# A gated attention and expert block on one core: the pieces of SP's, GpSimd's, ScalarE's, TensorE's and VectorE's lists set in another order

## The chip, the cores and the metric

One core of one Trainium2 chip. The metric is the device time of one launch in microseconds (us). The clock of TensorE has two levels here, 1.2 and 2.4 GHz; the profile gives the granted share of the higher one. In the tables PE is TensorE, DVE VectorE, ACT ScalarE, POOL GpSimd and SP the engine that only issues DMAs.

## The reference, cut to what matters

```python
# x (4, 512, 512), ctx (4, 512, 128), all float32; T = 4 * 512 rows
def mixer(h, adj, Wq, Wk, gamma_raw):                 # h = ctx, adj = layernorm(x)
    Q, K = heads(h @ Wq.T), heads(h @ Wk.T)           # 4 heads of 32
    sim = einsum('bhnd,bhmd->bnm', Q, K) / (sqrt(32) * 4)
    thr = top_k(sim, 153)[0][:, :, -1:]               # 153 = 0.3 * 512
    A = sigmoid(sim) * (sim >= thr)
    A = (A + swapaxes(A, -1, -2)) * 0.5
    g = sigmoid(gamma_raw)
    return (1 - g) * adj + g * A
def ffn(h, ...):                                      # h = layernorm(x), 8 experts, 2 of them per row
    shared = silu(h @ sg) * (h @ su) @ sd
    top_val, top_idx = top_k(h @ router, 2)
    probs = zeros.at[rows, top_idx].set(sigmoid(top_val))
    gate, up = split(einsum('etd,edf->etf', probs.T[:, :, None] * h, gate_up_w))
    return shared + einsum('eti,eid->etd', silu(gate) * up, down_w).sum(0)
x = x + tanh(g_xattn) * mixer(ctx, layernorm(x), ...)
x = x + tanh(g_ffn) * ffn(layernorm(x), ...)
```

## The kernel before, in words

The four blocks b of 512 rows go through the same stages, each of four tiles i of 128 rows. Every stage is a small helper, and each engine has a list of helper calls, written out by hand, that it works off strictly in order. Helpers of different engines meet in semaphores alone. So the order of the work is the five lists (SP's, GpSimd's, ScalarE's, TensorE's and VectorE's), and a helper that waits holds everything behind it in its list.

**Scores.** turn_ctx/turned_ctx (L926, L578) and turn_q/turned_q (L934, L582) make the operands, sim_tile (PE, L940) a 128x512 tile of scores, sim_of (ACT, L586) copies it to SBUF.

**Threshold search.** sim_stats (DVE) and spread (POOL) give a first probe; then four rounds k of count (DVE, L1385) and sign (ACT, L591), which count the entries above the probe for different tiles (block 0: two each; other blocks: DVE one, ACT three), and move (DVE, L1392), which sets the next probe. last_count, best_below and threshold (DVE, L1404 to L1436) end it; check_search stands on PE and DVE, read_bad on ACT. best_below works in two tiles of tmp which the one-hots use too, so it waits for the table before.

**Mixing.** value (ACT, L598) makes tanh and identity of four tiles, mask_sim (DVE, L1457) multiplies by the mask, affine (ACT, L620) scales x (with row_stats, row_affine on DVE, root_of_rows on POOL), turn_a (PE, L949) transposes the masked scores, add_own and add_turned (DVE) add them. mixed_stats, mixed_spread, normal_in (DVE), root_of_mixed (POOL) and normal (ACT, L626) are the second layer norm. The PE's turn_x2 (L960) and ACT's turned_x2 (L634) turn its rows.

**Routing and plan.** route, turn_logits (PE), turned_logits (ACT, L644); pick_experts (DVE, L1502) takes the logits, probs (ACT) and weigh_experts (DVE) the weights, which store_payload (SP) writes. rank_pairs (PE), rank_tokens (DVE, L1547) and one_hots (DVE, L1562: eight operations at L1569 and eight at L1572) are the operands of table (PE, L989), add_table (DVE) adds it up. count_pairs, order_columns, name_rows (PE) and sum_pairs, choose_columns, place_columns, read_plan (DVE) turn it into lists of rows. This is done twice: a first plan after blocks 0 and 1 gives the first nine groups of 128 rows (EARLY = 9), the second, after block 3, the other thirty. gather(t) (POOL, L477) fetches group t by an indirect DMA when rows and payload of its blocks are in DRAM.

**Jobs.** There are 55 jobs j. S jobs (the shared expert, one per tile of 128 rows) are j = 0 to 7, 12 to 15 and 19 to 22; M jobs (one expert on one gathered group t) are j = 8 to 11 (t = 0 to 3), 16 to 18 (t = 4 to 6) and from 23 on. Each is up(j) (PE, L1029), silu_of(j) (ACT), gate(j) (DVE, L1633), for an M job turn_h(j) and turned_h(j), then down(j) (PE, L1061), y_of(j) (ACT), and shared(j) or scatter(t) (POOL), which adds to the output in DRAM. up(j) waits for gate(j - 2); an S job's gate(j) waits for down(j - 2). An M job needs turn_rows(t) (PE, L1020) and turned_rows(t) (ACT) before. warm(n, count) (PE, L909) is `count` matmuls on ones that compute nothing.

From job 27 on the lists are loops of one M job a turn, alike in both kernels.

```python
            def best_below(b):
                ...
                if tables[0]:
                    dve.wait_ge(table_ps, tables[0])
            def gate(j):
                dve.wait_ge(silu_ready, j + 1)
                ...
                else:
                    if j >= 2:
                        dve.wait_ge(y_ps, j - 1)
```

## Time and profile before

| what | value |
|---|---|
| median of 3 runs | 416.89 us (416.11 to 417.19) |
| the profiled execution, its own time | 417.2 us |
| its span, first to last instruction | 415.5 us |
| mean granted clock | 0.976 |
| DVE, ACT, POOL busy | 182.1, 188.1, 132.0 us |
| SP's queue, GpSimd's queue | 28.40 MB, 24.81 MB |
| one job's 32 small matmuls of an S up / 4 matmuls of a down | 3.6 to 3.8 / 1.72 us |
| count of one tile, move, DVE | 0.74, 0.35 us |
| row_stats, sim_stats, DVE | 3.0, 2.0 us |
| last_count, best_below, threshold, DVE | 3.1, 4.8, 0.7 us |
| mask_sim or add_own, DVE | 2.7 us |
| add_turned, mixed_stats, DVE | 0.7, 0.7 us |
| mixed_spread, normal_in, DVE | 0.4 to 0.5, 0.15 us |
| pick_experts, rank_tokens, one_hots, DVE | 3.0, 1.2, 3.1 us |
| weigh_experts, row_affine, read_plan, DVE | 0.65, 0.6, 0.65 us |
| gate of an S job, of an M job, DVE | 0.41, 0.48 us |
| sim_of or turned_x2, sign (three tiles), value (two tiles), affine, ACT | 0.58, 2.2, 2.2, 2.9 us |
| normal, silu, y_of, turned_h, ACT | 0.75, 0.4, 0.68, 0.37 us |

The page gives the busy time of each engine and the chain of work that ended last; the views of stretches say in which part of the run an engine idles; the timeline gives single instructions with their start, their duration and, in brackets, how long the engine stood idle before and whose work ended that. The durations of pieces in the table are from the start of the piece to the start of the next in DVE's or ACT's timeline. The lists are in order, so such durations can be added up along a list, and a wait is the difference to what another list delivers.

### The profile page before, as it was taken

Reading aid. Unit: us, or ns where it says so; the run is one execution under the profiler, and the core shown is the slowest. Engines: PE = TensorE matmul, PEld = TensorE weight load, DVE = VectorE, ACT = ScalarE, POOL = GpSimd, SP = SyncE. Lnnn points to the kernel's source line nnn. Section 1 sums busy time; section 2 is a strip of 40 time slices with the busy share of each in tenths; the row PEclk is TensorE's granted clock in tenths of the full one; section 3 lists DMA queues with packets and bytes.
Section 4 is the critical chain, followed back from the end, with each engine's and each line's share of the span. In section 5 each row is a group of like instructions: output and inputs, shape, how many; then the busy total and the mean of one; then the engine's idle time right before and its main releaser. Section 6 shows DMA issues by size and latency. Waiting matters only on the chain.

```text
span 415.5 us, 5810 instructions
## 1 busy us (share of the span) xinstructions
PE 383.0 (92%) x1700; PEld 220.5 (53%) x1702; DVE 182.1 (44%) x746; ACT 188.1 (45%) x397; POOL 132.0 (32%) x124
## 2 busy tenths in 40 slices
PE   8939879968999989999999999999999999999980
PEld 4414576557855768576754444444444444444430
DVE  1898998999889889804500110111101110111000
ACT  3695885577366865154232432332323323333220
POOL 2100111010554234013420444444444444444321
PEclk9968999999999999999999999999999999999997
DMA  7999744373475463455350655555555444555332
GB/s 226 386 390 378 287 163 123 113 227 107 96 153 91 125 161 49 108 169 71 69 78 16 99 92 93 99 103 103 102 91 93 87 94 98 102 99 107 50 50 26
DMA packets 30469, 53.72 MB, mean 129 GB/s; under 512 B 4774, under 2 KB 8102, under 8 KB 30438
## 3 DMA queue, kind: packets, MB, share of 16 engines
q0 software_dynamic: 11040, 24.81, 34.2%
q1 hardware_dynamic: 19110, 28.40, 19.5%
q8 instruction: 15, 0.25, 0.2%
q10 hardware_dynamic: 288, 0.13, 0.1%
q14 instruction: 16, 0.13, 0.1%
HBM read 29.93 MB, written 23.40 MB: 128 GB/s over the span
## 4 chain that ended last, share of the span: by engine, by line
PE 76%; DVE 15%; issue 2%; DMA 2%; ACT 2%; POOL 1%; POOLq 0%; DVEq 0%
PE gate_up L1048 31%; PE down L1074 20%; PE gate_up L1044 9%; PE turned_x L1026 4%; DMA out_dram<-y_sb,idx 2%; PE down L915 2%; DVE ge_words L1388 2%; PE turned_h L1058 2%; DVE tmp L1572 2%; DVE tmp L1569 1%; PE front L963 1%; DVE statx L1348 1%; DVE xs L1479 1%; PE down L943 1%; PE front L953 1%
## 5 line engine op out<-in xcount | busy, mean ns | idle before, releaser
L1048 PE MATMUL gate_up<-w_gu,xT 128*128 x312 | 140.1, 593 | 0.0
L508 POOL DMA_INDIRECT out_dram<-y_sb,idx x39 | 62.1, 1593 | 112.3 <-DMA out_dram<-y_sb,idx 57.7
L1048 PEld LDWEIGHTS gate_up<-w_gu,xT 128*128 128x128 f32 x312 | 56.9, 190 | 59.8 <-issue 59.8
L1640 DVE SCALAR_TENSOR_TENSOR h<-gate_up,p_t,silu 128x256 f32<-128x256 f32 x39 | 18.9, 484 | 139.3 <-ACT silu L665 120.6
L1074 PE MATMUL down<-w_dn,hT 128*128 x156 | 73.5, 596 | 1.0 <-ACT hT L674 0.9
L1044 PE MATMUL gate_up<-xT,w_shgu 128*128 128x128 f32 x512 | 61.7, 281 | 2.0 <-ACT xT L642 1.1
L1044 PEld LDWEIGHTS gate_up<-xT,w_shgu 128*128 128x128 f32 x512 | 60.0, 196 | 4.1 <-issue 4.1
L692 ACT ACTIVATE y_sb<-down,gates 128x512 f32<-128x512 f32 x55 | 37.6, 686 | 49.7 <-PE down L1074 35.0
L665 ACT ACTIVATE silu<-gate_up,p_t 128x256 f32<-128x256 f32 x39 | 18.4, 473 | 77.4 <-PE gate_up L1048 74.2
L492 POOL DMA_INDIRECT xg<-x_rows,idx x39 | 40.1, 1028 | 37.6 <-DMA x_rows<-payl 18.6
L1074 PEld LDWEIGHTS down<-w_dn,hT 128*128 128x128 f32 x156 | 26.8, 190 | 21.8 <-issue 21.8
L594 ACT ACTIVATE junk<-sim,probe 128x512 int8<-128x512 f32 x44 | 31.2, 713 | 7.3 <-DVE probe L1379 5.3
L683 ACT COPY xT<-turned_x 128x512 f32<-128x512 f32 x39 | 22.8, 586 | 22.8 <-PE turned_x L1026 19.5
L475 POOL DMA_DIRECT2D out_dram<-y_sb x16 | 15.7, 979 | 51.3 <-ACT y_sb L692 51.3
L1074 PE MATMUL down<-w_shdn,hT 128*128 128x512 f32 x64 | 30.1, 597 | 0.0
L1026 PEld LDWEIGHTS turned_x<-ident,xg 128*128 128x128 f32 x156 | 19.2, 141 | 18.9 <-issue 18.7
L1630 DVE SCALAR_TENSOR_TENSOR p_junk<-xg,oh_e 128x8 f32<-128x8 f32 x39 | 6.2, 163 | 44.1 <-DMA xg<-x_rows,idx 40.2
L1026 PE MATMUL turned_x<-ident,xg 128*128 128x128 f32 x156 | 23.5, 273 | 0.5 <-issue 0.5
L1058 PEld LDWEIGHTS turned_h<-ident,h 128*128 128x128 f32 x78 | 10.6, 141 | 18.5 <-issue 15.3
L674 ACT COPY hT<-turned_h 128x256 f32<-128x256 f32 x39 | 14.2, 365 | 9.7 <-PE turned_h L1058 9.7
L1058 PE MATMUL turned_h<-ident,h 128*128 128x128 f32 x78 | 15.0, 274 | 1.1 <-DVE h L1640 1.1
L1074 PEld LDWEIGHTS down<-w_shdn,hT 128*128 128x128 f32 x64 | 11.1, 191 | 8.3 <-issue 8.1
(181 smaller groups left out, 396.3 us busy)
## 6 DMA issues: line engine op xcount, KB each, us to landing
w_gu<-in_L_ffn_gate_up_w_dram SPq DMA_DIRECT2D x8, 1024.0 KB, 12.3
xs<-in_x_dram SPq DMA_DIRECT2D x4, 1024.0 KB, 8.1
w_dn<-in_L_ffn_down_w_dram SPq DMA_DIRECT2D x8, 512.0 KB, 10.4
out_dram<-xs SPq DMA_DIRECT2D x4, 1024.0 KB, 4.3
x_rows<-x SPq DMA_DIRECT2D x4, 1024.0 KB, 5.5
out_dram<-y_sb POOLq DMA_DIRECT2D x16, 256.0 KB, 4.2
w_gu<-in_ctx_dram SPq DMA_DIRECT2D x4, 256.0 KB, 5.2
xg<-x_rows,idx POOLq DMA_INDIRECT x39
```

The source lines that it names most:

```text
L492: G.indirect_dma_start(out=xg[:, t % XG, :], out_offset=None, in_=x2_rows[0:2 * N, :] if t < EARLY else x2_rows[:, :], in_offset=bass.Indi ...
L508: G.indirect_dma_start(out=out[0:2 * N, :] if t < EARLY else out[:, :], out_offset=bass.IndirectOffsetOnAxis(ap=idx[:, t:t + 1], axis=0), ...
L594: ins = A.activation(junk[:, i - SHARE[b]], sim[:, b, i], ACT.Sign, scale=-1.0, bias=probe[:, k, i:i + 1], accum_out=sgn[:, k, i:i + 1])
L665: A.activation(silu[:, :], g_b[j % 2][:, 0:I], ACT.Silu, scale=p_t[:, t % XG:t % XG + 1]).then_inc(silu_ready, 1)
L683: A.copy(xT[:, x_slot(j)], x_b[:, :].rearrange("p (c t) -> p c t", c=DC)).then_inc(xt_done, 1)
L692: A.activation(y_sb[:, j % 2], y_b[j % 2][:, :], ACT.Copy, scale=gates[:, 1:2]).then_inc(y_done, 1)
L1026: mm = TE.transpose(x_b[:, c * P:(c + 1) * P], xg[:, t % XG, c * P:(c + 1) * P], ident[:, :])
L1044: mm = TE.matmul(g_b[j % 2][:, f * P:(f + 1) * P], w_shgu[:, c, f * P:(f + 1) * P], xT[:, x_slot(j), c], start=(c == 0), stop=(c == DC - 1))
L1048: mm = TE.matmul(g_b[j % 2][:, :], xT[:, x_slot(j), c], w_gu[:, bass.ds(experts[n] * (DC * F2) + c * F2, F2)], start=(c == 0), stop=(c == ...
L1058: mm = TE.transpose(h_b[:, c * P:(c + 1) * P], h[:, c * P:(c + 1) * P], ident[:, :])
L1074: mm = TE.matmul(y_b[j % 2][:, :], hT[:, j % 2, c], w, start=(c == 0), stop=(c == IC - 1))
L1640: V.scalar_tensor_tensor(h[:, :], g_b[j % 2][:, I:F2], p_t[:, t % XG:t % XG + 1], silu[:, :], ALU.mult, ALU.mult).then_inc(h_ready, 1)
```

## The change

Only the order of calls in the five lists changes; no helper is edited, and each call stands once in both. In the PE's list three waits for sim_ready (5, 6 and 10) are new and one for qT_ready (3) goes; the others move with the calls that they guard. The diff, cut to what the prediction speaks of:

```diff
@@ SP
+            load_x(1)
...
-            load_x(1)
-            load_shared()
             load_dn(4)
             load_dn(5)
+            load_shared()
...
+            store_rows(1)
+            store_payload(0)
             store_base(1)
             load_x(3)
-            store_rows(1)
+            store_payload(1)
             load_gu(7)
-            store_payload(0)
-            store_payload(1)
@@ GpSimd
+            spread(3)
+            gather(3)
             shared(3)
-            gather(3)
+            shared(4)
             gather(4)
...
             gather(6)
-            shared(6)
+            root_of_mixed(3)
             gather(7)
+            root_of_rows(3)
             shared(7)
-            root_of_mixed(3)
-            root_of_rows(3)
+            gather(8)
             scatter(0)
-            gather(8)
@@ ScalarE
             sign(0, 1)
+            turned_q(2)
             sign(0, 2)
+            sim_of(1, 0)
             sign(0, 3)
-            sim_of(1, 0)
+            value(0, (0, 1))
...
+            read_bad(0)
+            sim_of(2, 2)
+            affine(0)
+            value(0, (2, 3))
+            sign(1, 0)
             turned_ctx(3)
...
             turned_logits(0)
             read_bad(1)
+            affine(1)
             value(1, (0, 1))
...
             sim_of(3, 2)
+            y_of(2)
             turned_logits(1)
+            value(2, (0, 1))
             sign(2, 1)
@@ TensorE
-            pe.wait_ge(qT_ready, 3)
-            turn_q(3)
+            sim_tile(2, 0)
+            sim_tile(2, 1)
+            pe.wait_ge(sim_ready, 5)
+            sim_tile(2, 2)
+            pe.wait_ge(sim_ready, 6)
+            sim_tile(2, 3)
             pe.wait_ge(sim_ready, 8)
             check_search(0)
-            sim_tile(2, 0)
+            pe.wait_ge(sim_ready, 10)
             warm(1, 18)
-            sim_tile(2, 1)
-            sim_tile(2, 2)
             turn_a(0, 0)
...
             turn_a(0, 3)
-            sim_tile(2, 3)
-            sim_tile(3, 0)
+            turn_q(3)
...
             route(1)
+            pe.wait_ge(y_done, 2)
+            warm(4, 3)
             turn_logits(1)
             up(4)
+            rank_pairs(1)
             pe.wait_ge(logit_used, 2)
             count_pairs(0)
-            rank_pairs(1)
...
             table(0)
+            up(5)
             order_columns(0)
-            up(5)
+            down(3)
             pe.wait_ge(table_used, 1)
             table(1)
             name_rows(0)
...
             turn_logits(2)
+            up(12)
+            rank_pairs(2)
             up(13)
-            rank_pairs(2)
             down(10)
             down(11)
+            up(14)
             pe.wait_ge(rank_used, 3)
             table(2)
-            up(14)
+            up(15)
...
             count_pairs(1)
-            down(17)
-            down(18)
+            up(22)
             order_columns(1)
@@ VectorE
+            gate(3)
             mixed_spread(2)
-            gate(3)
+            rank_tokens(0)
+            normal_in(2)
+            weigh_experts(0)
+            one_hots(0)
             count(2, 0)
-            normal_in(2)
-            rank_tokens(0)
+            row_stats(2)
             move(2, 0)
-            weigh_experts(0)
-            row_stats(2)
-            one_hots(0)
-            row_affine(2)
-            count(2, 1)
             pick_experts(1)
             sum_pairs(0)
+            count(2, 1)
+            rank_tokens(1)
+            choose_columns(0)
             move(2, 1)
-            choose_columns(0)
-            rank_tokens(1)
             one_hots(1)
...
             mixed_spread(3)
+            normal_in(3)
+            weight_of(4)
+            row_stats(3)
+            gate(10)
+            row_affine(3)
...
+            weight_of(7)
+            count(3, 0)
+            move(3, 0)
+            count(3, 1)
+            pick_experts(2)
+            move(3, 1)
             count(3, 2)
+            rank_tokens(2)
             move(3, 2)
...
+            one_hots(2)
             gate(12)
+            count(3, 3)
+            move(3, 3)
             gate(13)
+            last_count(3)
```

Before, block 3's counts 0 and 1 stood between mask_sim(2) and add_turned(2, 1), and count(3, 2), count(3, 3) before pick_experts(2). The 55 jobs keep their numbers.

## Rows read from the trace of the kernel before

**Rows 1.** The page's busy time by engine: us, share of the span, instructions.
```profile
PE 383.0 (92%) x1700; PEld 220.5 (53%) x1702; DVE 182.1 (44%) x746; ACT 188.1 (45%) x397; POOL 132.0 (32%) x124
```

**Rows 2.** Four stretches: us, then busy us (instructions) of each engine, clock, DMA share, GB/s.
```profile
27.40:104.00 76.60, 67.14 (x431) 45.77 (x434) 70.41 (x295) 54.21 (x118) 8.46 (x9) 0.95 0.61 209
104.00:240.00 136.00, 133.52 (x718) 86.48 (x718) 77.14 (x299) 62.04 (x131) 44.20 (x39) 0.99 0.50 100
240.00:395.00 155.00, 155.00 (x480) 75.58 (x478) 16.80 (x81) 52.19 (x107) 70.39 (x54) 1.00 0.51 93
```

**Rows 3.** The PE's waits from 104 to 240: us in total, times, longest.
```profile
PE front L992 <- DVE tmp L1572: 1.1, 1, 1.1
PE front L1001 <- DVE el_b L1600: 0.7, 1, 0.7
PE turned_x L1026 <- issue: 0.5, 2, 0.3
```

**Rows 4.** Stretches around the two falls of the clock, columns as in rows 2.
```profile
20.50:27.00 6.50, 0.00 (x0) 0.00 (x0) 6.22 (x24) 5.69 (x14) 0.00 (x0) 0.74 1.05 386
...
92.00:95.00 3.00, 1.40 (x12) 0.86 (x13) 2.61 (x20) 3.00 (x8) 0.00 (x0) 1.00 0.55 113
...
99.00:102.00 3.00, 1.26 (x14) 1.12 (x15) 2.71 (x14) 2.10 (x7) 0.00 (x0) 1.00 0.17 31
102.00:105.60 3.60, 3.60 (x19) 3.60 (x19) 3.33 (x17) 0.51 (x2) 0.00 (x0) 0.53 0.09 9
```

**Rows 5.** The chain that ended last, in order of time: start, us, what.
```profile
101.95 8.87 PE gate_up L1044 x64
...
202.63 7.23 PE gate_up L1044 x64
```

**Rows 6.** The timeline of PE and DVE around the first turned tile of block 0.
```profile
31.75 4.92 PE L915 MATMUL down<-ones 128*128 128x512 bf16 x17 [0.22 <-issue]
...
39.80 0.75 DVE L1479 SCALAR_TENSOR_TENSOR xs<-front,c,xs 128x512 f32<-128x512 f32 x1 [1.29 <-PE front L956]
```

**Rows 7.** DVE's timeline: search, mixing, row statistics, logits, one-hots.
```profile
56.89 0.73 DVE L1407 TENSOR_SCALAR_CACHE_REDUCE ge_words<-sim,probe 128x512 uint8<-128x512 f32 x1
...
68.48 1.42 DVE L1461 SCALAR_TENSOR_TENSOR sim<-sim,thr,tmp 128x512 f32<-128x512 f32 x2 [0.66 <-ACT tmp L612]
...
79.31 0.17 DVE L1494 TENSOR_SCALAR pow2in<-mv 128x4 f32<-128x4 f32 x1
...
82.90 2.46 DVE L1348 BATCH_NORM_STATS2 statx<-xs 128x6 f32<-128x512 f32 x4
...
90.30 0.19 DVE L1508 COPY logit<-front 128x32 f32<-128x32 f32 x1
...
95.41 1.39 DVE L1569 TENSOR_SCALAR tmp<-iota_h,slot_f 128x128 f16<-128x128 f16 x8
...
96.72 1.88 DVE L1572 TENSOR_SCALAR tmp<-iota_h,slot_f,tok 128x128 f16<-128x128 f16 x8
```

**Rows 8.** The PE's timeline around the first plan: count_pairs(0) and name_rows(0).
```profile
93.60 0.16 PE L997 MATMUL front<-ones,msumx 128*128 128x1 bf16 x1 [1.94 <-DVE msumx L1590]
...
101.36 0.36 PE L1007 MATMUL front<-place,tab_f 128*128 128x9 f32 x2 [1.10 <-DVE tab_f L1585]
```

**Rows 9.** First gathers, the wait for gather(1), and the load of the last gate_up weights.
```profile
106.55 1.09 POOL L492 DMA_INDIRECT xg<-x_rows,idx  x1 [18.58 <-DMA x_rows<-payl]
...
109.77 1.53 POOL L492 DMA_INDIRECT xg<-x_rows,idx  x1 [0.30 <-issue]
...
113.88 0.17 DVE L1630 SCALAR_TENSOR_TENSOR p_junk<-xg,oh_e 128x8 f32<-128x8 f32 x1 [1.62 <-DMA xg<-x_rows,idx]
...
w_gu<-in_L_ffn_gate_up_w_dram SPq DMA_DIRECT2D x1, 1024.0 KB, 5.1
```

**Rows 10.** DVE's timeline: block 2's logits copied, block 3's mask.
```profile
147.04 0.19 DVE L1508 COPY logit<-front 128x32 f32<-128x32 f32 x1 [0.71 <-PE front L979]
...
162.65 2.74 DVE L1461 SCALAR_TENSOR_TENSOR sim<-sim,thr,tmp 128x512 f32<-128x512 f32 x4 [0.21 <-ACT tmp L612]
```

More of the change, by code:

```diff
@@ L718, in _ @@
             sim_of(1, 3)
-            turned_q(2)
-            turned_ctx(3)
-            value(0, (0, 1))
-            turned_q(3)
-            value(0, (2, 3))
-            sim_of(2, 0)
-            read_bad(0)
-            affine(0)
-            sim_of(2, 1)
-            sim_of(2, 2)
-            sign(1, 0)
+            sim_of(2, 0)
+            sim_of(2, 1)
+            read_bad(0)
[3 more added lines that the diff above has]
+            sign(1, 0)
+            turned_ctx(3)
             normal(0, 0)
-            normal(0, 1)
+            sign(1, 1)
             turned_x2(0, 0)
-            sign(1, 1)
             sim_of(2, 3)
             sign(1, 2)
-            turned_x2(0, 1)
-            silu_of(0)
-            sim_of(3, 0)
-            sign(1, 3)
+            normal(0, 1)
             normal(0, 2)
             normal(0, 3)
+            turned_x2(0, 1)
+            sign(1, 3)
+            silu_of(0)
+            turned_q(3)
             silu_of(1)
             turned_x2(0, 2)
-            affine(1)
             turned_x2(0, 3)
+            sim_of(3, 0)
             turned_logits(0)
             read_bad(1)
+            affine(1)
             value(1, (0, 1))
             value(1, (2, 3))
+            y_of(0)
             silu_of(2)
-            y_of(0)
             silu_of(3)
+            probs(0)
+            sim_of(3, 1)
+            sign(2, 0)
             y_of(1)
-            sign(2, 0)
-            sim_of(3, 1)
-            probs(0)
             normal(1, 0)
@@ L765, in _ @@
             sim_of(3, 2)
+            y_of(2)
             turned_logits(1)
+            value(2, (0, 1))
             sign(2, 1)
+            sign(2, 2)
             probs(1)
-            value(2, (0, 1))
+            sim_of(3, 3)
             silu_of(4)
-            sign(2, 2)
-            affine(2)
             silu_of(5)
@@ L829, in _ @@
             turned_rows(6)
+            y_of(14)
+            silu_of(17)
             normal(3, 0)
             normal(3, 1)
+            normal(3, 2)
+            turned_h(16)
+            normal(3, 3)
             turned_x2(3, 0)
-            silu_of(17)
-            normal(3, 2)
-            normal(3, 3)
-            turned_h(16)
             turned_x2(3, 1)
@@ L839, in _ @@
             turned_x2(3, 2)
-            turned_x2(3, 3)
-            y_of(14)
-            turned_logits(3)
-            turned_h(17)
             y_of(15)
             y_of(16)
+            turned_x2(3, 3)
+            turned_h(17)
             silu_of(19)
+            turned_logits(3)
             probs(3)
@@ L851, in _ @@
             silu_of(20)
-            silu_of(21)
             turned_rows(7)
             turned_rows(8)
+            silu_of(21)
             y_of(19)
-            y_of(20)
             silu_of(22)
-            turned_rows(9)
             silu_of(23)
             silu_of(24)
+            turned_rows(9)
+            y_of(20)
+            y_of(21)
             turned_rows(10)
-            y_of(21)
+            turned_h(23)
             y_of(22)
-            turned_h(23)
             turned_h(24)
@@ L1144, in _ @@
             turn_a(1, 3)
-            pe.wait_ge(logit_used, 1)
-            sim_tile(3, 1)
-            pe.wait_ge(y_done, 2)
-            warm(4, 3)
-            down(2)
+            down(1)
             pe.wait_ge(sim_ready, 14)
             rank_pairs(0)
-            down(3)
+            down(2)
             pe.wait_ge(at_used, 7)
@@ L1271, in _ @@
             name_rows(1)
-            up(21)
-            up(22)
             down(19)
@@ L1682, in _ @@
             normal_in(0)
-            add_turned(0, 2)
-            count(1, 1)
-            row_stats(1)
-            move(1, 1)
             add_turned(0, 3)
             mixed_stats(0, 2)
+            mixed_stats(0, 3)
+            count(1, 1)
+            mixed_spread(1)
+            move(1, 1)
+            row_stats(1)
+            normal_in(1)
             count(1, 2)
-            mixed_stats(0, 3)
             move(1, 2)
-            mixed_spread(1)
+            row_affine(1)
+            count(1, 3)
             sim_stats(2)
-            count(1, 3)
             move(1, 3)
-            row_affine(1)
-            normal_in(1)
             gate(0)
@@ L1734, in _ @@
             add_table(0)
-            gate(4)
-            move(2, 2)
             place_columns(0)
             add_table(1)
+            gate(4)
+            row_affine(2)
+            read_plan(0)
+            move(2, 2)
+            weigh_experts(1)
             count(2, 3)
-            read_plan(0)
             gate(5)
-            weigh_experts(1)
+            sim_stats(3)
             move(2, 3)
             last_count(2)
+            gate(6)
             best_below(2)
             weight_of(0)
+            gate(7)
+            threshold(2)
             weight_of(1)
-            gate(6)
-            sim_stats(3)
-            threshold(2)
-            gate(7)
             first_probe(3)
@@ L1798, in _ @@
             mask_sim(3)
+            gate(15)
             add_own(3)
```

204 lines of the change are left out of this document (95 added, 109 removed).

## The prediction, made blind

> **What bounds the kernel now.** I read the page's busy line first [rows 1]: the PE works 383.0 of 415.5 us, so its idle time and its slow time are the most that an order can win. The stretches [rows 2] say where that is. From 240 to 395 it has no gap at all (155.00 of 155.00), and the loop that runs there is not touched. From 27.4 to 104 it idles 9.5 us (76.60 less 67.14) while DVE is busy 70.4 of 76.6: that stretch is bound by DVE's list, with ACT behind it. From 104 to 240 the PE idles only 2.48 us. The PE's waits of over 0.2 us in that last stretch [rows 3] are 1.1 for the one-hots of block 2's table, 0.7 in the second plan, and 0.5 of "issue", in front of row turns, which stays whatever the order.
>
> Then the clock [rows 4]. Its mean is 0.74 over 20.5 to 27, in which the PE did nothing: it fell from full (2.4 GHz) to half (1.2 GHz) on the way. It falls again at 102, after a stretch in which the PE was busy 1.26 of 3.00 us, in short pieces. The chain [rows 5] prices that second fall: 64 matmuls of gate_up take 8.87 us behind 101.95 and 7.23 us behind 202.63, so 1.64 us. The PE goes from there to 240 nearly without a gap, so these 1.6 us reach the end whole.
>
> So the time of the end is: when the PE starts up(6) behind the first plan (101.80), plus what it loses to clock and waits after that.
>
> **The change, part by part.** Nothing is added, so no term is an operation; each is a piece that stands elsewhere.
>
> The durations of the pieces are those of the table in the section on the profile.
>
> *Block 0 (up to 57 us).* turned_q(2) and sim_of(1,0) (0.6 each) go between ACT's signs, where ACT stands still about 0.5 a round: some 0.2 us on the search. It lets sim_tile(2,*) run before warm(1,18), which then starts at top8's second tile (about 30.4), not at 31.75, and, with the clock as it was, ends near 36. In the trace DVE waited 1.29 us for turn_a(0,0), because the 17 warm matmuls and two sim tiles stood ahead of it [rows 6]; now it waits for mask_sim(0) alone (36.5). Gain at this point 1.3. It is mostly handed back: affine(0) (2.9 us) now stands ahead of value(0,(2,3)), which ends near 35.6, just in time for mask_sim's third tile; and the PE, with turn_q(3) behind turn_a(0,3) and waiting for turned_ctx(3) (behind sign(1,0)), does about 1.7 us of work between 41.6 and 47.5. I add DVE's pieces one behind the other, with the waits for sign, and get last_count(1) at 56.3 to 57.2, where it was at 56.89 [rows 7].
>
> *Block 1 to the first plan.* mask_sim(1) is tied to ACT: affine(1) (2.9) now stands behind read_bad(1), then four tanh and four identities. It ends at 69.2 to 69.8, before at 69.90 [rows 7]. mixed_spread(2) takes gate(3) ahead of it: 79.8, before 79.48. From there DVE had gate(3), count, normal_in, rank_tokens, move, weigh, row_stats, one_hots(0), row_affine(2) and count(2,1) before it copied block 1's logits at 90.30. Now it has 1.2 + 0.15 + 0.65 + 3.1 (the one-hots) + 0.75 + 3.0 + 0.35 = 9.2, so 89.0, and turn_logits(1), though behind y_of(2) and warm(4,3), is ready at about 88.6. Gain 1.3. Then pick 3.0, sum_pairs 0.2, count 0.75, rank 1.2, choose 0.35, move 0.35 = 5.9 (before 5.1): one_hots(1) at 94.9, over at 98.0, before 98.6. Gain 0.6. table(1) is now bound by the PE: up(4) 88.6 to 92.4, sim_tile(3,3) and table(0) to 94.2, up(5) to 98.0, then down(3) (1.72), which stood at 80 before. So table(1) ends at 100.4, DVE adds it by 100.8, name_rows(0) at 100.85, before 101.36 [rows 8]. **Term 1: 0.45 us**. It is all that the earlier plan wins, because down(3) fills the gap that the PE had (the 1.10 us in front of name_rows was a part of it).
>
> *The clock.* down(3), full matmuls, lies in just the stretch in which the PE had its short pieces. I expect no fall at 102. **Term 2: 1.6 us**; bounds 0 (it falls all the same) and 1.64. Against a sure gain speaks the stretch 92 to 95 [rows 4]: the PE was busy 1.40 of 3.00, hardly more than the 1.26 behind which the clock fell, and it held; the two rows alone do not tell why. With down(3) in it, 99 to 102 has some 2.5 of 3 and is nearer to the rows that held, so I take the 1.6. The same kind of lull is new at 41.6 to 47.5. A fall there slows up(0) by up to 1.7 us, but the search behind it is tied to DVE and ACT; it costs 0.9 at last_count(1), 0.55 at mask_sim(1) and is in the 0.3 that mixed_spread(2) is late above, so term 1 holds with it. The Trainium skill (TensorE: Matmul & The Clock Gate, Part 1) says that half clock is the default state and that activity releases it; by that rule the fall goes with the lull, to 41.6 to 47.5, and the sum stays as it is.
>
> *Rows of the first plan.* weigh_experts(1) ends at 103.4, 0.35 earlier; gather(0) then follows at about 106.2 (106.55) and can land by 110.3 if it takes what gather(1) took at most, 109.77 to 113.88 [rows 9]. The PE wants it earlier than it did: up(7) ends at 108.6, down(4) at 110.3 (before 112.5). No slack is left. And SP now sends load_gu(7), 1 MB, right behind payload(1), behind base(1) and load_x(3), where it went 9 us before the plan. I take 0.3 us of wait; bounds 0 and 2.7 (1 MB at the 386 GB/s of [rows 4]). **Term 3: -0.3**.
>
> *104 to 206.* I follow each wait of the PE by the same durations. Block 2's threshold is earlier (gate(6) and sim_stats(3) ahead of best_below(2), mask_sim(2) at 117.3, over 2 us earlier), and the mixing of block 2 is no longer cut by block 3's counts: mixed_spread(3) at 130.7, 4 us earlier. Block 3's counts come later, behind row_stats(3). New waits: turn_x2(2,3) for turned_x2(2,1), 0.4 us; name_rows(1) for add_table(3), 0.3. Gone: the 1.13 at table(2), since one_hots(2) ends at 150.5 while the PE has down(10), down(11) and up(14) until 155.8, and the 0.7 of order_columns(1), now behind up(22). Tight, by under half a us: up(9) for gate(7) (116.1 against 116.5), turn_x2(2,0), route(2), up(22) for gate(20). mask_sim(3) ends near 165.9 (before 165.39 [rows 10]) though the PE is 3 us ahead, so its slack shrinks by all of that. **Term 4: +1.13 + 0.7 - 0.7, and -0.3 for the tight ones = +0.8**; the rest of the 2.48 (0.5 "issue" and crumbs) I leave but for 0.4 that the re-cut 170 to 236 stretch saves. **Term 5: +0.4**. Beyond 206: gather(9) follows read_plan(1) (206.3, some 2.4 later than before) and lands near 210.5; turn_rows(9) is wanted at 216. Covered by down(19), down(20), up(23) and up(24); with that cover gone it would cost the 2.4 us whole.
>
> **Sum:** 0.45 + 1.6 - 0.3 + 0.8 + 0.4 = 2.95, say 3.0 earlier. The profiled execution took 417.2 (span 415.5); the median shown is 416.9, 0.3 under it. 417.2 - 3.0 - 0.3 = 413.9.
>
> **The rivals.**
> *A, forecast (0.56).* 413.9, between 412.3 and 415.4.
> *B, rows late (0.15).* The weight load and the gathers share the DMA engines; the gather's rows are 2 KB pieces scattered in DRAM. If the two run at once, turn_rows(0), and then turn_rows(1), wait up to 2.7 us instead of 0.3: 413.9 + 2.4 = 416.3, no change. For: the PE comes 2.2 us earlier, the data only 0.4. Against: in [rows 9] the same load, alone, lands in 5.1 us, so it is over by 108.5 to 109. The Trainium skill (DMA: Bandwidth & Descriptors, Queues, rings and completion order) has each engine alternate between the queues that have work; that rule speaks for B in kind, and its size would be a fair share, not the whole.
> *C, clock falls at 102 all the same (0.13).* Term 2 is gone: 415.5, just inside faster or no change.
> *D, slower (0.08).* pick_experts(2) now stands in DVE's list ahead of move(3,1), the rest of block 3's search, gate(12) and gate(13). It waits for turn_logits(2), which waits for ACT's turned_x2(2,3) behind normal(2,3), silu_of(11), y_of(8), turned_h(10), while the PE waits for turned_x2(2,1) from the same list. My time for the logits is 141.3 (before 147.0 [rows 10]), and up(14) has 1.1 us of slack for gate(12). Beyond that each us goes to the end one for one: L us late give 413.9 + L - 1.1, so from L = 4.1 on the kernel is slower than before, and at 6.5 it is 419.3. For it: three engines wait in a ring, and a count or gate that slips takes all. Against it: every piece of the ring has a row, and their sum from turn_x2(2,0) (133.1) to the logits is 8 us with no piece over 1 us, so 4 us more would need a wait I have not seen.
> *E, better than my losses (0.08).* Terms 3 and the tight ones vanish, the block 0 gain survives: 412.0.
>
> **Numbers.** The likeliest is A: 413.9. Range 411.6 to 416.8: from a little under E (whose terms are rounded to 0.1 and add up from four) to B with its full 2.7 us and the 0.2 that is left to it. Below 415.6 (0.3%, about what a measurement of this kernel can tell from no change) lie A, E and half of C: 0.72; within 0.3%: B, the rest of C and an edge of A: 0.19; above 418.1: D and a little: 0.09.
>
> **What would show it.** Right: one fall of the clock fewer behind 100 (windows), 64 matmuls behind name_rows in 7.2 us; block 1's logits copied near 89, the name_rows matmuls near 100.9; no PE wait for one_hots(2); the loop's start, read by any matmul of t = 12, 3 us earlier. Wrong: a PE wait in front of turned_x at 110 (B), a half clock at 102 (C), or new waits of the PE between 130 and 165 behind ACT or DVE (D). If DVE's list up to 80 us is over 1 us later than I have it, term 1 turns negative.

## The result, and the profile after

The changed kernel takes 411.93 us (median of 4 runs, 410.45 to 412.82) against 417.04 (4 runs, 416.11 to 417.30) for the kernel before, measured beside it: 0.9877 of its time, interval 0.9849 to 0.9905, so 5.1 us less. The forecast was 413.9, 3.0 us less. The sign and the range held; the gain was 2.1 us larger than the sum.

The profiled execution took 412.82 us with a span of 411.1; before, 417.2 and 415.5. This pair differs by 4.4, less than the medians, and one thing it holds against the changed kernel is that the first rows of x landed 0.9 later there. DVE's first row statistics show that; the timeline of DVE at the start, kernel before:

```profile
10.20 2.48 DVE L1348 BATCH_NORM_STATS2 statx<-xs 128x6 f32<-128x512 f32 x4 [2.28 <-DMA xs<-in_x_dram]
```

and after:

```profile
11.11 1.28 DVE L1350 BATCH_NORM_STATS2 statx<-xs 128x6 f32<-128x512 f32 x2 [4.06 <-DMA xs<-in_x_dram]
```

Over all traces of this study, of either order, this landing lies between 9.24 and 11.42, and everything behind it moves along. Where two traces are compared below, a time "from the landing" has it subtracted.

The busy line of the page after, then three stretches (columns as in [rows 2]):

```profile
PE 381.6 (93%) x1702; PEld 219.2 (53%) x1702; DVE 182.1 (44%) x746; ACT 187.0 (45%) x397; POOL 132.0 (32%) x124
```

```profile
27.40:104.00 76.60, 65.72 (x441) 46.40 (x442) 70.55 (x294) 51.24 (x115) 9.36 (x10) 0.95 0.61 200
104.00:240.00 136.00, 135.55 (x722) 86.93 (x721) 78.44 (x305) 65.12 (x137) 45.71 (x40) 1.00 0.51 108
240.00:390.00 150.00, 149.92 (x463) 73.07 (x461) 16.17 (x78) 51.00 (x104) 67.93 (x52) 1.00 0.51 93
```

Against [rows 2], the PE idles even more up to 104 (10.9 us, before 9.5), beside a DVE as full as before. From 104 to 240 its idle time is 0.45 us in place of 2.48, and one wait is left of those in [rows 3]:

```profile
PE turned_x L1026 <- issue: 0.4, 1, 0.4
```

So where did the time go? I read the start of the same piece in both traces; the last column has the 0.91 of the later landing added:

| piece, absolute start | before | after | earlier by | from the landing |
|---|---|---|---|---|
| turn_a(0,0) | 38.23 | 37.20 | 1.03 | 1.94 |
| turn_a(1,0) | 71.46 | 70.77 | 0.69 | 1.60 |
| name_rows(0) | 101.36 | 100.68 | 0.68 | 1.59 |
| turn_rows(0) | 112.38 | 110.07 | 2.31 | 3.22 |
| turn_rows(11) | 236.39 | 230.95 | 5.44 | 6.35 |
| end of the PE's last down | 405.53 | 400.29 | 5.24 | 6.15 |
| last scatter issued | 406.53 | 402.56 | 3.97 | 4.88 |

Two parts of this table were not in my sum: 3.1 us come between turn_rows(0) and turn_rows(11), where I had 1.2, and 1.3 us are lost again behind the PE's end.

### The profile page after: what moved, and what is told of

Its sections match the earlier page's. It is cut to its first block, busy times and chain, and to the rows that moved or that the text cites. A ratio compares the mean times of both kernels' runs of the same rounds, so it can differ in the third digit from the quotient of the medians.

```text
span 411.1 us, 5817 instructions
## 1 busy us (share of the span) xinstructions
PE 381.6 (93%) x1702; PEld 219.2 (53%) x1702; DVE 182.1 (44%) x746; ACT 187.0 (45%) x397; POOL 132.0 (32%) x124
## 4 chain that ended last, share of the span: by engine, by line
DMA 38%; PE 34%; issue 10%; DVE 7%; ACT 5%; POOL 1%; POOLq 1%; SPq 1%; DVEq 0%; ACTq 0%
DMA out_dram<-y_sb,idx 36%; PE gate_up L1044 14%; PE down L1074 8%; PE gate_up L1048 6%; DMA xs<-in_x_dram 2%; PE front L953 1%; DVE statx L1350 1%; PE front L963 1%; ACT junk L594 1%; PE turned_x L1026 1%; DMA xg<-x_rows,idx 1%; POOL out_dram L475 1%; ACT sim L589 1%; PE front L956 1%; ACT y_sb L692 1%
```

## The experiments

The experiments fall into three sets, each on a chip of its own, with the kernel before beside it: experiments 1 to 4 (417.51 us, 19 runs), experiments 5 to 7 and the first run of 11 (420.45, 11 runs), and experiments 8 to 10 and the second run of 11 (420.28, 11 runs). Medians are compared within a set; across sets only the ratios are.

**1. The changed kernel again.** No edit.

> The changed kernel once more. All theories: near 411.9 us, about 5 us under the kernel before. No fall of the clock near 100, matmuls of up(6) and up(7) together 7.2 us. If the last scatters are issued one right behind the other (each waiting for the one before and none for y_of), the end is set by the chain of scatters, not by the PE; if one of the last three waits for y_of, by the PE.

411.98 us (4 runs, 411.44 to 412.64), ratio 0.9874 (0.9855 to 0.9893). The gain of 5.1 to 5.5 us stands. The last eleven scatters each wait for the one before and none for y. But the trace differs in one place from the first one of the same kernel: the PE's clock. Stretches after, in the first trace:

```profile
47.80:53.30 5.50, 5.45 (x34) 5.48 (x35) 5.26 (x21) 4.67 (x10) 1.29 (x2) 0.69 0.64 245
...
99.00:102.00 3.00, 2.47 (x22) 1.88 (x21) 2.31 (x15) 0.39 (x1) 0.00 (x0) 1.00 0.02 5
102.00:105.60 3.60, 3.60 (x35) 3.60 (x34) 3.43 (x15) 2.85 (x8) 0.00 (x0) 1.00 0.21 47
```

and up(0) in its PE timeline, then the same piece when the kernel ran again:

```profile
47.85 5.44 PE L1044 MATMUL gate_up<-xT,w_shgu 128*128 128x128 f32 x32 [1.91 <-issue]
```

```profile
47.05 3.81 PE L1044 MATMUL gate_up<-xT,w_shgu 128*128 128x128 f32 x32 [1.91 <-issue]
```

In the first trace the clock fell to half (1.2 GHz) behind the lull in front of up(0), which the prediction had named as a possible place; in the second it stayed at full speed behind the same lull of 1.91 us. From the landing of x, name_rows(0) starts at 89.57 with the fall and at 88.49 without: the fall costs 1.1 us at the first plan. One kernel, two behaviours: a fall seen in one trace isn't yet a property of the order.

**2 and 3. The halves.** The lists of both kernels are cut behind the first plan: SP's after load_gu(7), payload(1), GpSimd's after gather(6), shared(6), ScalarE's and TensorE's after row turns 2, VectorE's after mask_sim(2). One kernel has the new order up to the cut and the old one behind it, the other the reverse. The core of it in VectorE's list, against the changed kernel:

```diff
             mask_sim(2)
+            count(3, 0)
             gate(8)
+            move(3, 0)
...
-            count(3, 0)
-            move(3, 0)
-            count(3, 1)
             pick_experts(2)
```

and, as it turned out to matter, where weight_of(5) stands:

```diff
             mixed_stats(2, 0)
+            weight_of(5)
             mixed_stats(2, 1)
...
             row_affine(3)
-            weight_of(5)
```

New up to the cut (experiment 2):

> New order up to the first plan, mask_sim(2) and turn_rows(2), old order behind. Theory of my terms: terms 1 and 2 alone, 0.45 to 0.7 plus 1.6, so 2.0 to 2.5 us under the kernel before (about 414.7), and the PE's waits for table(2) (1.1) and order_columns(1) (0.7) come back. Rival (the new part behind the plan is what counts, since DVE's later list is what freed the PE): less than 1 us under before. Rival (chain of scatters caps both halves): over 3.5 us under before, nearly the whole gain.

417.69 us (12 runs, 415.61 to 420.25), ratio 1.0016 (0.9993 to 1.0039): nothing is won, where terms 1 and 2 promised 2.0 to 2.5. Its PE reaches turn_rows(0) at 110.05, as early as in the changed kernel, and turn_rows(4) at 146.27, as late as before (146.25). From the landing a lead of 3.1 us becomes one of 0.8; the PE's waits of this kernel from 104 to 240:

```profile
PE front L963 <- ACT x L631: 1.9, 1, 1.9
PE front L992 <- DVE tmp L1574: 1.1, 1, 1.1
PE front L1001 <- DVE el_b L1602: 0.8, 1, 0.8
```

and its timeline at the first:

```profile
137.12 1.34 PE L963 MATMUL front<-ident,x 128*128 128x128 f32 x8 [1.89 <-ACT x L631]
```

The PE stands 1.9 us in front of turn_x2(2,0), for the second layer norm of block 2. That comes off DVE's list, and there this kernel has a wait that comes from its seam alone. The new list of GpSimd has gather(5) behind shared(6), so it goes at 126.44 (before: 116.59); the old list of VectorE has weight_of(5), which reads its rows, between the pieces of block 2's mixing. GpSimd's and VectorE's timelines of this kernel:

```profile
126.44 1.07 POOL L492 DMA_INDIRECT xg<-x_rows,idx  x1 [0.30 <-issue]
```

```profile
130.65 0.17 DVE L1632 SCALAR_TENSOR_TENSOR p_junk<-xg,oh_e 128x8 f32<-128x8 f32 x1 [2.24 <-DMA xg<-x_rows,idx]
```

Neither the kernel before nor the changed kernel waits at that place. An estimate from these rows: 2.24 us earlier the operand of turn_x2(2,0) is there at 134.9, and the PE, free at 135.2, doesn't wait. So this run doesn't show that the old lists hand the early lead back, nor that block 3's counts in them do. What the early half is worth ahead of the old lists, without the seam's wait, stays open.

New behind the cut (experiment 3):

> Old order up to the first plan, mask_sim(2) and turn_rows(2), new order behind. Theory of my terms, corrected by the trace after: 2.0 to 2.8 us under the kernel before (about 414.6), with the clock at half around 102 to 105.6 and up(6), up(7) in 8.9 us, and no PE wait over 0.5 us from 104 to 200. As forecast (terms 3 to 5, 0.9): about 416.1. Rival (the halves need each other: new order behind with DVE late runs into waits): same as before or slower.

414.85 us (8 runs, 413.79 to 416.30), ratio 0.9943 (0.9924 to 0.9962): 2.7 us less. In its trace turn_rows(0) to turn_rows(11) takes 121.90 us; before 124.01, after 120.88. So the late half is worth 2.7 by itself, and the early half, ahead of the new late lists, the difference of this kernel to the changed one: 414.85 to 411.98, 2.9 us. The prediction had 1.2 for the late half (terms 4 and 5) and 1.75 for the early one (terms 1 to 3). Its PE also had one wait for rows:

```profile
PE turned_x L1026 <- DMA xg<-x_rows,idx: 0.5, 1, 0.5
```

**4. Without down(3) in the lull.**

```diff
             rank_pairs(0)
+            pe.wait_ge(y_done, 2)
+            warm(4, 3)
             down(2)
+            down(3)
...
             route(1)
-            pe.wait_ge(y_done, 2)
-            warm(4, 3)
...
             order_columns(0)
-            down(3)
             pe.wait_ge(table_used, 1)
```

> The changed kernel with down(3) and warm(4,3) back where they stood, around down(2). Theory of term 2: the PE is left with short pieces again before name_rows(0), the clock falls near 100 and up(6), up(7) take 8.9 us; name_rows itself at most 0.3 earlier: 1.3 to 1.6 us slower than the changed kernel. Rival (the earlier data alone keep the clock up, down(3) is no matter): within 0.5 us of the changed kernel and no fall of the clock near 100.

412.23 us (6 runs, 410.27 to 414.45), ratio 0.9890 (0.9868 to 0.9912): 0.25 us from the changed kernel, nothing that can be measured. Its stretches, around where down(3) was:

```profile
95.00:99.00 4.00, 2.24 (x24) 1.92 (x23) 3.77 (x17) 1.73 (x7) 0.00 (x0) 1.00 0.60 232
99.00:102.00 3.00, 3.00 (x27) 3.00 (x28) 2.73 (x18) 1.71 (x4) 0.00 (x0) 1.00 0.03 5
```

The lull is back (2.24 of 4.00 us busy), and no fall follows it. name_rows(0) even starts 0.6 us earlier from the landing (87.89 against 88.49), as table(1) no longer waits for down(3).

**5. The kernel before again, a single run,** on the second chip.

> The kernel before, profiled once more. If the fall of the clock at 102 belongs to the old order, it is there again and turn_rows(0) comes 11.0 us behind name_rows(0); if it hangs on where in time the lull falls, it can be gone (9.4 us).

419.59 us. Its stretches:

```profile
92.00:95.00 3.00, 1.20 (x8) 0.66 (x9) 2.63 (x18) 3.00 (x9) 0.00 (x0) 1.00 0.73 173
95.00:99.00 4.00, 4.00 (x28) 4.00 (x26) 3.81 (x21) 4.00 (x9) 0.00 (x0) 0.57 0.52 184
99.00:102.00 3.00, 2.47 (x27) 2.31 (x26) 2.68 (x13) 1.47 (x5) 0.00 (x0) 1.00 0.39 117
102.00:105.60 3.60, 3.60 (x33) 3.60 (x34) 3.21 (x17) 1.30 (x4) 0.00 (x0) 1.00 0.09 9
```

Behind the lull of [rows 4] that had held the clock (1.40 of 3.00 us busy, here 1.20) it fell, and at 102, where it had fallen, it is 1.00. The half clock lies on up(5) here, ahead of the plan, and the plan is no later for it: name_rows(0) starts at 90.89 from the landing, in the other trace at 91.16. name_rows(0) to turn_rows(0) takes 9.39 us, in the trace of before 11.02. What that gives is still there further on: from the landing this execution is 1.9 us ahead of the other one at turn_rows(0) (100.28 against 102.18), 1.7 at turn_rows(4) (134.37 against 136.05) and 1.5 at turn_rows(11). The last scatters can't be compared, as the chips differ.

**6. The kernel before with down(3) moved alone, a single run.**

```diff
             rank_pairs(0)
-            down(3)
...
             up(5)
+            down(3)
             pe.wait_ge(table_used, 1)
```

> The kernel before with one call moved: down(3) behind up(5), ahead of table(1), as in the changed kernel. Theory of term 2: no fall of the clock at 102, up(6) and up(7) in 7.2 us; turn_rows(0) 1.6 us less behind name_rows(0) than before (11.0). The end hardly moves (under 0.5 us), because the old lists behind it hand the gain back, as in the run with the new order up to the first plan. Rival (down(3) is no matter): the clock falls there as in the kernel before.

421.63 us, within the 417.96 to 422.96 of the kernel before in this set. No fall at 102 (its only one behind 40 us lies at 59 to 62), and 9.38 us from name_rows(0) to turn_rows(0). turn_rows(4) comes at 135.4 from the landing, against 134.4 in experiment 5, which has no fall at 102 either, and 136.1 in the trace of before, which has it. One run doesn't say whether the move gains anything at the end.

**7. The lull at up(0) filled:** 13 more empty matmuls.

```diff
             turn_a(0, 3)
+            warm(5, 5)
             turn_q(3)
             pe.wait_ge(at_used, 3)
             turn_x2(0, 0)
+            warm(6, 8)
```

> The changed kernel with 13 more empty matmuls where the PE stands idle in block 0 (5 ahead of turn_q(3), 8 behind turn_x2(0,0)), 2.8 us of work that fit into its idle time there. Theory: they keep the clock up, so up(0) takes 3.6 us in every execution and not 5.4, and turn_a(1,0) comes 27.2 us behind turn_a(0,0)'s mask or less, as in the execution of the changed kernel without that fall; in the median 0.3 to 0.8 us faster than the changed kernel, if the end follows the PE. Rival (the chain of scatters sets the end): the turns of the rows come earlier but the end stays within 0.3 us. Rival (they get in the way): slower by up to 1 us.

414.29 us (6 runs, 413.43 to 415.68), ratio 0.9850 (0.9814 to 0.9886); the changed kernel has 0.9868 (0.9840 to 0.9895) on the third chip (experiment 9). up(0) runs at full clock (3.81 us), name_rows(0) starts at 88.61 from the landing, as in the unfilled kernel when its clock holds. The end doesn't tell the two apart.

**8. Both: down(3) back and the lull filled.** The edits of 4 and 7 together.

> The changed kernel with down(3) and warm(4,3) back around down(2), and the 13 empty matmuls in block 0's idle time. Each alone kept the clock up at up(0) in its profile, or made name_rows(0) 0.5 us earlier. Theory: 0.3 to 0.8 us under the changed kernel, with turn_rows(0) at most 97.5 us behind the first row statistics. Rival (chain of scatters takes it): turn_rows(0) as early, the end within 0.3.

413.90 us (5 runs, 413.79 to 414.60), ratio 0.9852 (0.9826 to 0.9878), beside 414.14 for the changed kernel in the same set. turn_rows(0) comes at 97.57 from the landing, 0.3 to 0.4 earlier than in the two traces of the changed kernel without a fall (97.87, 97.95). 0.24 us is within the noise: no version here beats the changed kernel for sure.

**9. The changed kernel on the third chip.** No edit.

> The changed kernel, as the measure of this call: near 0.987 of the kernel before.

414.14 us (6 runs, 412.45 to 415.94), ratio 0.9868 (0.9840 to 0.9895). It is the reference for 8, 10 and the second run of 11.

**10. Block 3's counts 0 and 1 back between the pieces of block 2's mixing,** with their signs:

```diff
@@ VectorE
             mask_sim(2)
+            count(3, 0)
             gate(8)
+            move(3, 0)
             add_own(2)
+            count(3, 1)
             add_turned(2, 0)
+            move(3, 1)
...
-            count(3, 0)
-            move(3, 0)
-            count(3, 1)
             pick_experts(2)
-            move(3, 1)
@@ ScalarE
             turned_rows(2)
+            sign(3, 1)
...
             y_of(9)
-            sign(3, 1)
```

> The changed kernel with count(3,0), move(3,0), count(3,1), move(3,1) back between mask_sim(2) and add_turned(2,1), and ACT's sign(3,1) back behind turned_rows(2). Theory (the old order of 104 to 146 is bound by DVE and ACT, not by the PE; these pieces stand ahead of block 2's mixing): normal(2,0) comes 2 us later, the PE waits 1.5 to 2.5 us for it in front of turn_x2(2,0), and the end is 1.5 to 2.3 us later than the changed kernel's. Theory as forecast (each wait of the PE priced by itself, block 2's mixing no term): under 0.5 us. Rival (the scatters set the end): the wait is there and the end moves by less than 0.8.

415.81 us (6 runs, 415.15 to 416.38), ratio 0.9896 (0.9872 to 0.9919): 1.7 us more than the changed kernel in the same set. The PE's waits from 104 to 240:

```profile
PE front L953 <- DVE xs L1481: 0.9, 2, 0.6
PE turned_x L1026 <- issue: 0.4, 1, 0.4
```

The mechanism is the one expected, but it bites a step earlier, at turn_a(2, ...) and not at turn_x2(2,0). turn_rows(3) to turn_rows(4) takes 19.98 us, in experiment 9 18.63. This one move of the change is worth 1.35 us in the trace and 1.7 at the end; the prediction noted it ("no longer cut by block 3's counts") and gave it no price.

**11. The PE delayed** behind turn_rows(11), by nine empty matmuls ahead of the loop:

```diff
             down(25)
+            pe.wait_ge(table_used, 4)
+            for _ in range(9):
+                TE.matmul(f_b[0][:, :], ones[:, :], ones[:, 0:1].to_broadcast([P, N]), start=True, stop=True)
             for j in range(27, NJ - 6):
```

> The changed kernel with 9 empty matmuls (1.94 us) ahead of up(27), in front of the loop; nothing else moves. If the PE sets the end: 1.9 us slower than the changed kernel (about 413.9). If the chain of scatters sets the end, which catches up by about 0.4 us a job: slower by less than 1.2 us, and the last scatters wait for y_of where they waited for the scatter before.

416.03 us (6 runs, 413.44 to 416.97), ratio 0.9886 (0.9848 to 0.9925). The changed kernel wasn't in this set. Experiment 7 was, and against its 414.29 this is 1.7 us more, what a PE that sets the end would give; but the six runs spread over 3.5 us and the intervals of the two ratios overlap. It was made again beside experiment 9:

> Again the 9 empty matmuls (1.94 us) ahead of up(27), now beside the changed kernel on the same chip. PE sets the end: 1.9 us slower than the changed kernel. Scatters set it: under 1.2 us. Both in part (the chain of scatters just catches up): 1.2 to 1.7.

414.48 us (6 runs, 413.60 to 416.74), ratio 0.9871 (0.9842 to 0.9901): 0.34 us more than the changed kernel. The delay is there, in the PE's timeline:

```profile
231.67 1.91 PE L1297 MATMUL front<-ones 128*128 128x512 bf16 x8
```

and turn_rows(11) to turn_rows(12) takes 7.77 us for 5.81. The PE ends at 400.38, 1.95 later than in experiment 9 (398.43), but 0.87 of that is there at turn_rows(11) already, ahead of the delay: of 1.96 us of delay only 1.08 are left at the PE's own end. The last scatters in GpSimd's timeline of experiment 9:

```profile
396.42 1.55 POOL L508 DMA_INDIRECT out_dram<-y_sb,idx  x1 [3.96 <-DMA out_dram<-y_sb,idx]
401.80 1.55 POOL L508 DMA_INDIRECT out_dram<-y_sb,idx  x1 [3.83 <-DMA out_dram<-y_sb,idx]
```

and with the delay:

```profile
397.64 1.55 POOL L508 DMA_INDIRECT out_dram<-y_sb,idx  x1 [4.12 <-DMA out_dram<-y_sb,idx]
403.06 1.55 POOL L508 DMA_INDIRECT out_dram<-y_sb,idx  x1 [3.87 <-DMA out_dram<-y_sb,idx]
```

In both each scatter waits for the one before it, not for y. The delayed kernel's last scatter is 1.26 later in this pair of traces, of which 0.9 lies already in its first one (228.31 against 227.44), ahead of the delay. So in this pair of traces 1.94 us of PE time in the loop come to about 0.4 us at the last scatter: there the chain of scatters sets the end, not the PE. The medians agree (0.34) but don't settle it, as their intervals are about 1.2 us to either side, and the first run, against experiment 7, went the other way.

## Why the prediction was right, and where its sum was not

**Term 1 (0.45 us at name_rows(0)): near the pair's 0.68 by luck, and too small.** DVE's timeline after, against [rows 7]:

```profile
57.23 0.73 DVE L1409 TENSOR_SCALAR_CACHE_REDUCE ge_words<-sim,probe 128x512 uint8<-128x512 f32 x1
...
68.23 1.42 DVE L1463 SCALAR_TENSOR_TENSOR sim<-sim,thr,tmp 128x512 f32<-128x512 f32 x2 [0.53 <-ACT tmp L612]
...
79.68 0.17 DVE L1496 TENSOR_SCALAR pow2in<-mv 128x4 f32<-128x4 f32 x1
...
89.28 0.19 DVE L1510 COPY logit<-front 128x32 f32<-128x32 f32 x1 [0.26 <-issue]
...
94.96 1.39 DVE L1571 TENSOR_SCALAR tmp<-iota_h,slot_f 128x128 f16<-128x128 f16 x8
```

I had 56.3 to 57.2 for the first, 79.8 for the third, 89.0 for the logits and 94.9 for the one-hots, so up to 0.3 us off. That is luck in part: my sums start from the trace of before, whose landing is 0.9 earlier. From the landing my times for the last three are 0.6 to 1.0 us too late against this trace and 1.7 to 2.1 against experiment 1, which has no fall at up(0). The matmuls of the plan, where I had 100.85 for the second (compare [rows 8]):

```profile
92.58 0.16 PE L997 MATMUL front<-ones,msumx 128*128 128x1 bf16 x1 [0.20 <-DVE msumx L1592]
...
100.68 0.36 PE L1007 MATMUL front<-place,tab_f 128*128 128x9 f32 x2 [0.53 <-DVE tab_f L1587]
```

The prediction counted in absolute time, and the late landing of x (0.9) and the fall at up(0) (1.1) were inside the measured 0.68. From the landing the lead is 1.3 to 1.6 with that fall and 2.3 to 2.7 without (91.16 and 90.89 in the two traces of before; 89.57 with the fall, 88.49 and 88.57 without in those of the changed kernel). "It costs 0.9 at last_count(1), 0.55 at mask_sim(1) and is in the 0.3 that mixed_spread(2) is late" held the fall for the normal case and a little too cheap: last_count(1) and mask_sim(1) start 46.1 and 55.2 from the landing with it and 45.1 and 54.2 without, so 1.0 each.

**Term 2 (1.6 us, the clock at 102): seen in the pair, but the fall at 102 isn't a fixed cost of the old order, and the new one doesn't need down(3) to be rid of it.** The chain of waits after, against [rows 5]:

```profile
101.27 7.25 PE gate_up L1044 x64
```

8.87 became 7.25, 1.62 of the 1.64. But experiment 5 has the kernel before with its fall at 95, where it doesn't delay name_rows(0), and in experiment 3 it is the same (90.59 from the landing); experiments 4 and 8 have the new order without down(3) in the lull and still no fall. Over all traces, a fall from 94 on came in all three with the old order up to the plan, one of them at 102; none came between 94 and 106 in the one that had down(3) moved alone (experiment 6), nor in any of ten with the new order, two of which have down(3) elsewhere. So down(3) may be enough in the old order (one trace), and in the new one something else keeps the clock there. How often the kernel before has its fall at 102 the few traces can't say, so what term 2 is worth in the median isn't known. Nor do the runs settle the step "The PE goes from there to 240 nearly without a gap, so these 1.6 us reach the end whole": the two traces of the kernel before speak for it as far as turn_rows(11) (1.5 us left there, experiment 5), and experiment 2, where the lead is lost, has its seam's wait in it. At turn_rows(0) terms 1 to 3 promised 1.75, and the lead from the landing is 3.2 in the pair and 2.3 to 2.4 between experiment 5 and the unslowed traces of the changed kernel (100.28 against 97.87 and 97.95): there the sum was near because term 1 was too small while term 2 counted a fall that doesn't always come. The Trainium skill (TensorE: Matmul & The Clock Gate, Part 1) makes half clock the default that activity lifts; the fall at up(0) in the first trace goes with that, and the same lull with the clock held in the second shows that the lull's length alone doesn't settle it.

**Term 3 (-0.3, rows of the first plan): too careful by 0.3.** GpSimd's timeline and the DMA issues after, against [rows 9]:

```profile
105.81 1.12 POOL L492 DMA_INDIRECT xg<-x_rows,idx  x1 [15.72 <-DMA x_rows<-payl]
```

```profile
w_gu<-in_L_ffn_gate_up_w_dram SPq DMA_DIRECT2D x1, 1024.0 KB, 5.5
```

The gather went at 105.81 (I had 106.2), the load that shares the engines with it took 5.5 us (alone before: 5.1), and turn_rows(0) waited for nothing. Rival B's mechanism was seen once, in experiment 3, with 0.5 us. The Trainium skill's rule of engines alternating between queues (DMA: Bandwidth & Descriptors, Queues, rings and completion order) fits the 0.4 us that the load got longer, in one trace each; a wait of B's size came in no trace.

**Terms 4 and 5 (+1.2 us, 104 to 240): the term that was mis-sized.** turn_rows(0) to turn_rows(11) went from 124.01 to 120.88 us, so 3.1. Idle time of the PE is 2.0 of it: the waits for the one-hots and for order_columns went, as forecast, and none of the 1.0 us of new waits and tight spots came. The other 1.1 is in no wait that the view lists; the PE's busy time in that stretch fell from 121.53 to 120.43. 0.2 of it is one turn_h that the new order has behind turn_rows(11): at turn_rows(12) the lead is 5.24. The rest are shorter records of the same matmuls, 0.6 of it on the 80 of down, which I can't place. My times for the lists came out 0.1 to 0.5 us off, again with the later landing in them; from the landing they are 0.8 to 1.4 too late. DVE's timeline after, against [rows 10], where I had 130.7, 141.3 and, for the first operation of the mask, 163.1:

```profile
130.25 0.17 DVE L1496 TENSOR_SCALAR pow2in<-mv 128x4 f32<-128x4 f32 x1
...
141.44 0.19 DVE L1510 COPY logit<-front 128x32 f32<-128x32 f32 x1 [1.91 <-issue]
...
163.18 2.74 DVE L1463 SCALAR_TENSOR_TENSOR sim<-sim,thr,tmp 128x512 f32<-128x512 f32 x4 [0.54 <-ACT tmp L612]
```

What was mis-sized is the price. I charged the stretch with the PE's idle time of before, 2.48 us at most, and took 1.0 of that back for new waits that didn't come. The new late lists gain more than that idle time. By themselves they are worth 2.7 us at the end (experiment 3), 2.1 of it from turn_rows(0) to turn_rows(11) in its trace (121.90 us against 124.01). And they let a PE that comes earlier keep its lead, which the old idle time can't show, as it is measured with a PE that comes late. Experiment 10 measures one such piece: with block 3's counts back between block 2's mixing, where in the kernel before no wait of the PE stood behind them, the changed kernel waits 0.9 us for add_turned and ends 1.7 later. The prediction had no term for it.

Experiment 2 looks as if the whole lead were lost to the old lists, since its PE idles 4.69 us in this stretch, the old 2.48 and 2.2 on top:

```profile
104.00:240.00 136.00, 131.31 (x704) 83.77 (x703) 77.22 (x302) 65.00 (x135) 42.89 (x38) 1.00 0.50 105
```

But 1.9 of that is the wait behind gather(5) at its seam, and in experiment 5, whose PE comes to turn_rows(0) 1.9 us earlier from the landing than in the trace of before, the old lists make it idle 2.74 us from there to turn_rows(11), 0.26 more than 2.48. How much of an early lead the old lists would take is open.

**What the sum left out: the tail.** Before, the page's chain of what ended last was 76% PE and 2% DMA. After, the chain, and from the costliest groups the scatter:

```profile
DMA 38%; PE 34%; issue 10%; DVE 7%; ACT 5%; POOL 1%; POOLq 1%; SPq 1%; DVEq 0%; ACTq 0%
...
L508 POOL DMA_INDIRECT out_dram<-y_sb,idx x39 | 62.1, 1592 | 112.6 <-DMA out_dram<-y_sb,idx 79.5
```

The last scatters before, in GpSimd's timeline, still waited for y twice of three times:

```profile
395.94 1.55 POOL L508 DMA_INDIRECT out_dram<-y_sb,idx  x1 [3.81 <-ACT y_sb L692]
401.40 1.55 POOL L508 DMA_INDIRECT out_dram<-y_sb,idx  x1 [3.90 <-DMA out_dram<-y_sb,idx]
406.53 1.55 POOL L508 DMA_INDIRECT out_dram<-y_sb,idx  x1 [3.58 <-ACT y_sb L692]
```

and after, none:

```profile
391.91 1.55 POOL L508 DMA_INDIRECT out_dram<-y_sb,idx  x1 [3.76 <-DMA out_dram<-y_sb,idx]
397.04 1.55 POOL L508 DMA_INDIRECT out_dram<-y_sb,idx  x1 [3.58 <-DMA out_dram<-y_sb,idx]
402.56 1.55 POOL L508 DMA_INDIRECT out_dram<-y_sb,idx  x1 [3.97 <-DMA out_dram<-y_sb,idx]
```

Between scatter(7), the first behind 226 us, and the last lie 31 steps; they took 171.6 us before (234.95 to 406.53) and 172.4 after (230.18 to 402.56), 5.54 and 5.56 a step. The lead of the first is 4.8, that of the last 4.0, while the PE ends 5.2 us earlier and then has nothing to do. That the end has gone over from the PE to the scatters holds for these executions and isn't a line between the two orders: of the last eleven scatters none waits for y in experiment 5, which is the kernel before on another chip, and three of the last four do in experiment 4, a new order. The two chains end close together. The prediction said of this stretch only that it isn't touched. Its measure, the loop's start "3 us earlier", came out at 5.2 (turn_rows(12) at 236.76 against 242.00).

**The rivals.** A had the sign and the range, and the measured 411.93 lies 0.1 us under E. What E names did come: turn_rows(0) waited for no rows, the tight spots cost nothing, and the gain of block 0, 1.94 at turn_a(0,0) from the landing, is still 1.6 at turn_a(1,0), with the fall at up(0) in between. Its number is right by luck, as it has neither the 2.7 us of the late half nor what the tail takes back. B, C (no fall at 102 in any trace of the new order) and D didn't happen. The ring of D held: the logits of block 2 came 0.14 us from my time; from the landing they are 0.8 ahead of it.

## What to carry to other kernels

Price a stretch by the list that binds it: take the arrival of the others as fixed, move the waiting engine by the lead you expect, and read the new wait. Its idle time in the trace of before is only what is left after it came late; experiment 10 has 1.7 us of cost where that trace has no wait. If a change has an early and a late part, test them apart, but look in the traces of the halves for waits that neither whole kernel has: here one of 2.2 us at the seam made the early half look worthless. Compare traces from a common event, here the landing of x, before a time that comes out right is called right. And before an engine at 100% is called the bound up to the end, look whether a serial chain of transfers runs beside it at nearly the same pace.

## What the runs showed of the hardware

- **Falls of the clock move between executions of the same kernel.** The kernel before has one at 102 in one trace and at 95 in the other; with the new order up to the plan, four of the eight traces that have the 1.91 us of idle time ahead of up(0) have one there, four have none, and neither have the two in which it is filled (experiments 7 and 8). The two that are priced here cost 1.6 us each: 32 matmuls in 5.44 for 3.81 at up(0), 64 in 8.87 for 7.25 at 102. Why it falls behind one lull and not behind an equal one stays open: neither the length of the lull nor its busy share separates the cases (in a stretch of 3.00 us the PE was busy 1.26 and 1.20 us where the clock fell behind, and 1.40 and 1.07 us where it held).
- **A chained scatter has a pace of its own.** 128 rows of 512 f32, added to DRAM, each issued when the one before has landed: 5.53 to 5.58 us a step on average in the six traces of the result and the first set, 5.63 to 5.66 in the eight on the two other chips, of which 1.55 to 1.6 is the issue. Whether two chains side by side would free more wasn't tried.
- **Chips differ by 3 us** (417.5 on one against 420.5 and 420.3 on two others for the same kernel), more than half of this change; the changed kernel's ratio is the same on the first and the third (0.9874 and 0.9868).
- **The first rows of x land at 9.2 to 11.4 us**, in any order of the lists, and the rest of the execution moves with it.
